# A software pipeline over 32 batches: setup turned into steps with slots of their own, and every step placed anew

## The reference, cut to what matters

```python
c_proj = silu(c) @ W_mod + b_mod
shift_a, scale_a, gate_a, shift_m, scale_m, gate_m = split(c_proj, 6)
q, k, v = split(modulate(ln(x), shift_a, scale_a) @ W_qkv + b_qkv, 3)      # 16 heads of 16
x = x + gate_a * (attention(q, k, v) @ W_proj + b_proj)
q_c = ln(x) @ W_qc + b_qc
k_c, v_c = split(ln(context) @ W_kvc + b_kvc, 2)
x = x + attention(q_c, k_c, v_c) @ W_cproj + b_cproj
h = gelu(modulate(ln(x), shift_m, scale_m) @ W_mlp1 + b_mlp1) @ W_mlp2 + b_mlp2
return x + gate_m * h
```

## Time and profile before

| what | value |
|---|---|
| three executions | 1495.04, 1495.16, 1497.20 us; median 1495.16 |
| the profiled execution | 1498.68 us, span of its trace 1496.5 us |
| mean granted PE clock | 0.976 of 2.4 GHz |
| busy, share of the span | PE 92%, DVE 74%, ACT 73%, POOL 47% |
| chain that ended last | PE 70%, DVE 10%, DMA 8%, ACT 3%, POOL 3% |

### The profile page before, as it was taken

One profiled execution on the slowest core, in us unless ns is written; L12 is line 12 of the kernel. 1 busy time (PEld: TensorE's weight loads), 2 busy tenths in 40 slices (PEclk: granted clock), 3 DMA queues, 4 the chain that ended last, 5 costly groups with the idle time before them and its releaser, 6 DMA issues.

```text
span 1496.5 us, 39974 instructions
## 1 busy us (share of the span) xinstructions
PE 1379.4 (92%) x15090; PEld 908.1 (61%) x15090; DVE 1111.4 (74%) x1992; ACT 1094.9 (73%) x1852; POOL 708.3 (47%) x995
## 2 busy tenths in 40 slices
PE   3567899999999999999999999999999999999877
PEld 1334566666666666666666666666666666665545
DVE  4647877788777777787777787887777777875535
ACT  3145787777788887777788887787788877877653
POOL 2233344455545544555545544555455544555421
PEclk8689999999999999999999999999999999999989
DMA  5122233333332333333333233333332333332111
GB/s 178 45 78 87 88 95 95 96 109 98 98 93 94 94 95 99 99 109 96 94 96 94 91 99 99 100 108 93 92 99 90 97 95 96 109 95 68 59 32 35
DMA packets 142132, 137.97 MB, mean 92 GB/s; under 512 B 38069, under 2 KB 116566, under 8 KB 141942
## 3 DMA queue, kind: packets, MB, share of 16 engines
q1 hardware_dynamic: 141942, 135.42, 29.1%
HBM read 56.34 MB, written 9.55 MB: 44 GB/s over the span
## 4 chain that ended last, share of the span: by engine, by line
PE 70%; DVE 10%; DMA 8%; issue 3%; ACT 3%; POOL 3%; SPq 2%; DVEq 0%; ACTq 0%; POOLq 0%
PE dense_ps L348 14%; PE dense_ps L349 12%; PE dense_ps L350 12%; PE o_ps L696 11%; PE max_ps L661 10%; PE exp_ps L678 6%; DMA o_rb_cross<-r_dram_cross 4%; DVE mx_cross L1015 4%; PE dense_ps L596 4%; DVE mx_self L1015 2%; DMA r_dram_cross<-o_r_cross 2%; ACT probs L818 1%; SPq L433 1%; POOL o_n_cross L1150 1%; POOL Y L1179 1%
## 5 line engine op out<-in xcount | busy, mean ns | idle before, releaser
L818 ACT ACTIVATE probs<-exp_ps 128x1024 f32<-128x1024 f32 x512 | 525.9, 1027 | 185.7 <-PE exp_ps L678 183.2
L1015 DVE TENSOR_REDUCE mx_cross<-max_ps 128x4 f32<-128x1024 f32 x256 | 313.3, 1224 | 100.2 <-PE max_ps L661 92.4
L1015 DVE TENSOR_REDUCE mx_self<-max_ps 128x4 f32<-128x1024 f32 x256 | 312.3, 1220 | 75.8 <-PE max_ps L661 73.4
L1150 POOL TENSOR_TENSOR o_n_self<-o_n_self,o_rb_self 128x512 f32<-128x512 f32 x32 | 40.6, 1269 | 295.9 <-DMA o_rb_self<-r_dram_self 295.9
L1183 POOL TENSOR_TENSOR g_split<-G,g_split 128x512 f16<-128x512 f32 x120 | 136.7, 1161 | 58.1 <-ACT g_split L807 58.1
L348 PE MATMUL dense_ps<-xt,mlp_hi 128*128 128x256 f16 x512 | 139.8, 273 | 3.0 <-DVE xt L979 2.8
L348 PE MATMUL dense_ps<-mlp_hi,g_split 128*128 128x256 f16 x504 | 139.6, 277 | 1.1 <-DVE g_split L1093 1.1
L350 PE MATMUL dense_ps<-xt,mlp_lo 128*128 128x256 f16 x512 | 139.6, 273 | 0.0
L349 PE MATMUL dense_ps<-xt,mlp_hi 128*128 128x256 f16 x512 | 139.5, 273 | 0.0
L350 PE MATMUL dense_ps<-mlp_hi,g_split 128*128 128x256 f16 x504 | 138.9, 276 | 0.0
L349 PE MATMUL dense_ps<-mlp_lo,g_split 128*128 128x256 f16 x504 | 138.9, 276 | 0.0
(11 more groups left out here) (230 smaller groups left out, 3338.0 us busy)
## 6 DMA issues: line engine op xcount, KB each, us to landing
q_stack_self<-split_q SPq DMA_DIRECT2D x192, 64.0 KB, 2.6
k_stack_self<-split_k SPq DMA_DIRECT2D x192, 64.0 KB, 2.6
k_stack_cross<-split_kc SPq DMA_DIRECT2D x192, 64.0 KB, 2.6
q_stack_cross<-split_qc SPq DMA_DIRECT2D x192, 64.0 KB, 2.6
X<-in_x SPq DMA_DIRECT2D x32, 256.0 KB, 2.8
Ctx<-in_ctx SPq DMA_DIRECT2D x32, 256.0 KB, 3.3
rows_a<-rows_a_dram SPq DMA_DIRECT2D x32, 256.0 KB, 3.3
o_n_self<-o_sb_self SPq DMA_DIRECT2D x64, 128.0 KB, 2.8
```

What stands on the lines that cost most here:

```text
L818: nc.scalar.activation(probs[:, t % 8:t % 8 + 2], exp_ps[:], ACT.Exp).then_inc(exp_taken[kind], 2)
L1015: nc.vector.tensor_reduce(mx[kind][:, :, :, t // 2].rearrange("p q a -> p a q"), max_ps[:].rearrange("p a (q k) -> p a q k", q=2), AX_X, A ...
L1150: nc.gpsimd.tensor_tensor(o_n[kind][:], o_n[kind][:], o_rb[kind][:], ALU.mult).then_inc(o_mult[kind], 1)
```

## The change

Setup becomes 36 steps with slots in a table `FOLD`, and each engine's `at` issues them in the slot order together with the steps of the batches. The assertions on `FOLD` only keep semaphore counts in order. SP loads the first third of `W_mod`, then `W_qkv`, `x` of batch 0 and `b_mod`, then the rest. The eight columns of `b_qkv` are issued on ACT's queue, behind its first exponent. PE runs 36 matmuls on an identity before it has data. `PLAN` is changed in about half its entries, and `AHEAD` covers batches 0 to 6 and 25 to 31 in full (before: 0 to 2 and 28 to 31, in part).

```diff
 PLAN = {
...
-    "v_hi": (-1, 1, 11), "split_self": (0, 0, 15), "m_self": (0, 1, 1), "m_copy_self": (0, 1, 2),
-    "o_gather_self": (1, 0, 11), "o_recip_self": (1, 0, 12), "r_out_self": (1, 0, 15), "r_back_self": (1, 1, 1),
-    "o_norm_self": (1, 1, 1), "o_hi_self": (1, 1, 3), "o_lo_self": (1, 1, 4), "rows_a": (0, 1, 1),
+    "v_hi": (-1, 1, 11), "split_self": (0, 1, 0), "m_self": (0, 1, 1), "m_copy_self": (0, 1, 2),
+    "o_gather_self": (1, 0, 13), "o_recip_self": (1, 0, 12), "r_out_self": (1, 0, 13), "r_back_self": (1, 0, 13),
+    "o_norm_self": (1, 0, 13), "o_hi_self": (1, 1, 3), "o_lo_self": (1, 1, 5), "rows_a": (0, 1, 2), "xr": (0, 1, 14),
...
-    "norm2": (2, 0, 1), "t2": (2, 0, 2), "t2_hi": (2, 0, 2), "t2_lo": (2, 0, 3), "qc": (2, 0, 5),
+    "proj": (1, 1, 6), "x2": (1, 1, 9), "x2_add": (1, 1, 12), "ln2": (1, 1, 13), "norm2": (1, 1, 15),
...
-    "g_hi_1": (4, 1, 4), "g_hi_2": (4, 1, 6), "g_hi_3": (4, 1, 8), "g_lo_0": (4, 1, 10), "g_lo_1": (4, 1, 10),
-    "g_lo_2": (4, 1, 10), "g_lo_3": (4, 1, 11), "mlp2_0": (4, 1, 13), "mlp2_1": (4, 1, 15), "mlp2_2": (5, 0, 1),
+    "g_hi_0": (4, 1, 4), "g_hi_1": (4, 1, 6), "g_hi_2": (4, 1, 7), "g_hi_3": (4, 1, 10), "g_lo_0": (4, 1, 9),
+    "g_lo_1": (4, 1, 9), "g_lo_2": (4, 1, 11), "g_lo_3": (4, 1, 14), "mlp2_0": (4, 1, 13), "mlp2_1": (4, 1, 15),
...
 AHEAD = {
-    0: {"exp_self": -1, "load_x": 9, "ln1": 12, "norm1": 18, "t1": 8, "t1_hi": 8, "t1_lo": 8, "q": 8, "q_hi": 7,
+    0: {"max_self": 1, "load_x": 68, "ln1": 42, "norm1": 98, "t1": 34, "t1_hi": 82, "t1_lo": 39, "q": 35, "q_hi": 38,
+        "q_lo": 37, "stack_q": 49, "k": 30, "k_hi": 31, "k_lo": 36, "stack_k": 32, "v": 31, "v_hi": 25,
...
-    2: {"m_self": 1, "tc": -3, "stack_kc": 5, "g_hi_3": 1, "g_lo_2": -5, "g_lo_3": -4, "mlp2_0": -2},
+    2: {"load_x": -15, "ln1": 4, "norm1": 26, "t1": -2, "t1_hi": 1, "q_hi": 2, "q_lo": -5, "stack_q": -5, "k": 3,
...
+FOLD = {
+    "mod_0": -349, "mod_0_out": -175, "mod_0_turn": -112, "mod_0_split": -146, "hi_qkv": -268, "lo_qkv": -73,
+    "q_bias": -54, "q_bias_out": -60, "hi_mlp1": -206, "hi_kvc": -150, "hi_proj": -142, "hi_qc": -74,
+    "hi_cproj": -34, "hi_mlp2": -21, "lo_mlp1": -63, "lo_kvc": -41, "lo_proj": -29, "lo_qc": -27, "lo_cproj": -26,
+    "lo_mlp2": 15, "mod_rest": -68, "mod_add": -56, "mod_turn": -50, "shift_split": -50, "columns": -48,
+    "shift": -26, "shift_out": -9, "row_v": -25, "row_v_out": -9, "row_c": -8, "row_c_out": -5, "gate": -7,
+    "gate_out": 2, "rows_out": -14, "row_back": -14, "k_ones": -21, "v_ones": -54}
...
+        for step, slot in FOLD.items():
+            self.steps[step, slot] = Batch(0)
...
 SP
-            nc.sync.dma_start(cnd, cond).then_inc(setup_in, 16)
+            nc.sync.dma_start(cnd, cond).then_inc(cond_in, 16)
...
+            nc.sync.dma_start(wm[:, 0:2 * D], wm_dram[:, 0, 0:2 * D]).then_inc(mod_in, 16)
+            nc.sync.dma_start(wm2[:, 0:2 * D], wm_dram[:, 1, 0:2 * D]).then_inc(mod_in, 16)
...
+            load_weight("qkv")
+            nc.sync.dma_start(X[:, 0], x[0:1].rearrange("a (t p) d -> p (a t) d", p=P)).then_inc(x_in[0], 16)
...
+            nc.sync.dma_start(wm[:, 2 * D:6 * D], wm_dram[:, 0, 2 * D:6 * D]).then_inc(mod_rest_in, 16)
+            nc.sync.dma_start(wm2[:, 2 * D:6 * D], wm_dram[:, 1, 2 * D:6 * D]).then_inc(mod_rest_in, 16)
+            for name in W_ORDER[1:]:
                 load_weight(name)
...
             def load_rows(b, dst, src, s):
+                sp_wait(rows_stored, 16 * 5 if b.n == 0 else 0)
...
 PE
-            pe.wait_ge(ident_made, 1)
+            pe.wait_ge(ident_made, 2)
+            fill(o_ps[:, 0], 36)
             pe.wait_ge(dve_set, 1)
...
-            pe.wait_ge(dve_set, 5)
-            pe.wait_ge(w_lo_done, 1)
...
+            def mod_rest():
+                pe.wait_ge(mod_rest_in, 16 * 2)
...
+                if kind == "self" and b.n == 0:
+                    pe.wait_ge(dve_set, dve_value["gate_out"])
...
 ACT
-            act.wait_ge(setup_in, 16 * 4)
+            act.wait_ge(cond_in, 16)
             nc.scalar.activation(cexp, cnd, ACT.Exp, scale=-1.0).then_inc(act_set, 1)
-            for name in EARLY_W:
-                split_weight(name)
...
+                        nc.scalar.dma_start(b_qk_col[64 * a:64 * a + 64, n * C + c:n * C + c + 1], stacked_bias(b_qkv, n * D, a, c)
...
             def keep_values(b, unit, kind):
                 act.wait_ge(ready[unit], b.n + 1)
+                if b.n == 0:
+                    act.wait_ge(v_ones, 1)
...
 POOL
+            def v_ones_set():
+                pool.wait_ge(pe_set, pe_value["mod_rest"])
...
```

507 lines of the change are left out of this document (356 added, 151 removed), and 40 rows, old and new, of tables (AHEAD, PLAN).

## The result

| what | before | after |
|---|---|---|
| median of four executions each | 1496.18 us (1495.04 to 1498.78) | 1534.69 us (1532.52 to 1537.48) |
| ratio | | 1.0256, 95% interval 1.0233 to 1.0279 |
| the profiled execution | 1498.68 us | 1535.65 us |

The change makes the kernel 2.6% slower; I had forecast 1483 us.

A forecast was written before the change was run, and what follows sets the result against it. PE was taken to bound the middle, leaving gains at the ends: 11.4 us at the front plus 1.0 in the filling, 12.4 off 1495.2, gives 1482.8, said as 1483 us; range 1470 to 1490.

The forecast's parts named there:

- The first maximum: Front: DVE's first row maximum comes at 42.0 us instead of 54.12, 12.1 us won, bounds 39 and 45.
- The middle: Batches 5 to 31, bound by PE: 0 us won, at 42.0 to 42.3 us per batch; bound 7.5 won.
- the rival that makes it faster: Middle: disturbances go, 42.27 us per batch falls to 41.98, total 1475.5 us; chance 0.05.
- the one with `g_lo_3` in front of `norm2`: POOL, every middle batch: a delay beyond 3.2 us of slack slows all 27 batches, 1510 us at 1 us excess; chance 0.07.
- The tail behind batch 31: Stretch from batch 31's copy of the row maxima to the end: as long as before, 143.6 us, within 3 us.
- Step 1: Setup loads: the 2.5 us hole in transfers goes, ACT's split of `W_kvc` begins at 16.9 instead of 18.71; bounds 14.2 and 19.4.
- The later steps: Front after the loads: batch 0's transposed input done at 20.8, low half of k at 29.6, first maximum at 42.0 us.
- New waits: Steps queued behind newly placed ones around the first batches: together 0.7 us lost, leaving 11.4 won past batch 1.
- The rest of the filling: Batches 1 to 6: maxima and exponents keep their order, 1.0 us won; bounds 11 won and 3 lost.
- The tail: Last batches: gains from `cproj(29)` and about 1 us lost at batch 31's reciprocals, sum 0, bounds 3 us either way.
- The gain doesn't arrive: Rival: chains of transfers in the first batches give back half or all of the gain, 1489 to 1495 us; chance 0.10.
- The test that I set for myself: Forecast is wrong if the first maximum is early but batch 5's copy of the row maxima, expected near 241.6 us, isn't.

The follow-up runs named there:

- columns_later: The changed kernel with the eight columns of `b_qkv` issued on SP, behind all weight loads but the last, and none on ACT; 1538.23 us.
- end_as_before: The changed kernel with the steps of batches 25 to 31 in the slots they had before; 1516.44 us.
- filling_as_before: The changed kernel with batches 2 to 6, and what setup doesn't need of 0 and 1, in the slots of before; 1505.20 us.
- loads_behind: The changed kernel with nine 256 KB transfers of the filling moved behind the fetch of the sums; 1538.12 us.
- queue_as_before: The changed kernel with stacks, gathers, reciprocals, `r_out` and `r_back` of batches 2 to 6 and 25 to 31 in the slots of before; 1589.18 us.
- setup_alone: The kernel before with only the new setup and new places up to the first maximum of batches 0 and 1; 1493.72 us, ratio 0.9985.

## Why the prediction was wrong

**What held.** The first maximum, the last of my sums for the front: forecast 42.0 with bounds 39 and 45, measured 44.02, so 10.1 of 12.1 us; in part this is luck, since its first step came later than its bound and the others made some of it good (next paragraph). In the other runs with this setup it comes between 41.41 and 45.29. The middle: 42.2 us per batch from 7 to 24; neither the rival that makes it faster nor the one with `g_lo_3` in front of `norm2` shows there. The tail behind batch 31: 2.5 us shorter (to the end of the trace, as I had counted, 141.0 instead of 143.6), inside the 3 us that I gave.

**Step 1, mis-sized.** I took the hole of 2.5 us as won whole and expected the split of `W_kvc` at 16.9. The timeline of ACT in the kernel after:

```profile
21.28 2.23 ACT L959 ACTIVATE kvc_hi<-o_sb_self 128x64 f16<-128x64 f32 x9 [1.73 <-DMA o_n_cross<-in_L_xcond_W_cproj]
...
23.93 0.82 ACT L979 ACTIVATE xt<-dense_ps,cols_a_all 128x256 f16<-128x256 f32 x2
```

It is 1.9 us beyond even my later bound, 19.4; in the other runs with these loads it is 19.19 to 21.54. I had taken the rate outside the hole, 390 GB/s, for granted; measured are 230 to 303 from 3.75 to 9.75 us. The later steps gave back 2.4 of these 4.4 us. The Trainium skill, "DMA: Bandwidth & Descriptors", section "Issuing engines are not separate DMA queues", by which I reckoned the first maximum 2.5 us later, at 44.5, was nearer to it. The trace agrees with that in the number and not in the mechanism: the hole is gone, and a lower rate has taken its place. `columns_later`, with no column on ACT, has the same rates, so the place of the columns was not where this time could be won.

**New waits, mis-sized.** I priced what stands behind the first maximum at 0.7 us. Batch 0's copy has 8.0 of the 10.1 left, batch 1's 6.2, batch 2's 1.0. One piece is a row that I had not looked for: `split_self(0)` on DVE took 2.60 us instead of 0.17 beside POOL's `k_ones` (below).

**The rest of the filling: the step that failed.** I wrote 1.0 won, with 3 lost as the other bound, for which I gave no row, and reasoned that maxima and exponents keep their order while dense steps move by some slots. The measurement is 35.3 us lost between batch 0's copy and batch 7's. I had counted the waits that the new places remove and not the ones that they add: of some 60 steps in each of seven batches the question is what stands behind it on its engine, and I had asked that for the setup and batch 1 alone. The way of the sums could have been read from the trace of before: 10.5 to 13.4 us from the last copy of the outputs to the product. The new places put the product's reader ahead of an exponent on ACT, and stacks ahead of the gather on SP. Which engine's order carries the loss stays open: DVE's new order among the old ones loses as much as all five, giving back the other four takes nothing away, and the run that gives back DVE's alone is missing.

**The tail, failed too.** Sum 0 with 3 either way, but I looked at batches 29 to 31 and behind. The 13.8 us are lost between the copies of 24 and 31, 7.1 of them by the copy of 28, by places of batches 25 to 31 that I priced at nothing (`end_as_before`).

**The rivals.** The slower one had the right kind, a step late in front of others on an in-order engine, and the wrong place: POOL in the middle, at 0.07. "The gain doesn't arrive" ended at 1495, no more than the gain given back. The test that I set for myself, first maximum early and batch 5 not, is what happened: 267.15 instead of 241.6.

**Shown and not shown.** Shown: both losses belong to the places of the first and last seven batches (`filling_as_before`, `end_as_before`); about 18 of 27 us in the filling hang on the way of the sums (one pair without it); setup and steady part together are a small gain, and the setup alone has as much within the intervals. Not shown: a single place, or a single engine's order, that costs most of the filling. The runs that give back engine by engine, `loads_behind` and `queue_as_before` say that there may be none, since each mixture of old and new orders makes waits of its own, and by this they are weak as a test of any one place. Why the same places lose 23 us in one execution and 34 in another stays open, too.

## What to carry to other kernels

A hand-placed software pipeline is one order over all engines. Before a step is moved, the time that every wait in it needs is read from the trace (here 10.5 to 13.4 us from the last output to the product), and what stands behind it on its in-order engine: a step put nearer to its input than that waits, with everything queued behind it. Re-placed stages are best timed and kept stage by stage: here setup and middle alone give 0.998, with filling and end 1.026. An early start is worth only what the next stage keeps: in `setup_alone` 10.3 us at the first maximum are 2 in the median.

## What the runs showed of the hardware

**A short stall can cost twice.** The stretches of the filling with stalls ran at a granted clock of 0.96 to 0.97 on average, where before had 1.00. In each of them the clock fell once from its upper level, 2.4 GHz, to the lower, 1.2 GHz: at 295.74 us, as PE's idle 3.48 us ended, and at 227.47 and 346.94 us, 1.4 and 1.0 us after PE had been idle for 2.42 and 2.33 us. Batches 4 to 7 have 1400 matmuls in 130.2 us of busy time, the same three of before 1406 in 125.3. So of the 20.5 us lost there, 15.5 are idle time (16.9 instead of 1.4) and some 5 a slower PE. My sum had no such term. Not every stall did this: after 2.16 us of idle time (to 310.11 us), and in the end after 2.48 us (to 1184.76 us), the clock stayed at its upper level, and the stretch from 26 to 27 has a mean of 1.00.

**DVE and POOL hold each other up.** Timelines of DVE and POOL in the kernel after:

```profile
60.10 2.60 DVE L1229 TENSOR_SCALAR mh_self<-mx_self 128x32 f16<-128x32 f32 x1
```

```profile
59.15 3.51 POOL L1386 MEMSET k_stack_cross<- 128x4096 f16 x1
```

The same operation takes 0.17 us elsewhere (at 214.92); here it ends with the memset, at 62.7. In the other runs with this setup it takes 1.1 to 3.2 us in this place. In the other direction POOL's `norm1` took 2.79 us at 16.93, and 1.10 elsewhere, beside DVE's split of `W_qkv` from 15.38 to 18.74. The Trainium skill, "SBUF — State Buffer", section "Who interferes with whom", says that the two engines share a pair of ports, which, for certain forms of DVE's instructions, the first to issue holds for its whole instruction while the other waits. The first pair of rows agrees. The second agrees in part: the first of `norm1`'s two instructions took 2.24 us and ended 0.4 us behind the split, but the split is 17 instructions, and POOL's outlasted the last eight of them and not only one.
